# Two deformable convolution layers on one core: the order of dense tiles in the mixed stages, and the waits at the entry of the second convolution

## The reference

```python
def _deform_sample(x, offset):          # per image, tap k of 9, pixel (y, x)
    py = y + ky + off_y; px = x + kx + off_x
    # bilinear: four corners of (py, px), weights (1-|py-iy|)*(1-|px-ix|), 0 outside

# layer 0
offset = conv3x3(xn, w_off) + b_off                 # 18 channels
z = einsum('bckhw,ock->bohw', _deform_sample(xn, offset), w_dcn) + b_dcn
x = x + relu(batchnorm(z))

# layer 1, identity = xn = _gn(x)
out = gelu(batchnorm(modulated_deform_conv(xn, offset1, mask1, w_dcn1)))
out = batchnorm(modulated_deform_conv(out, offset2, mask2, w_dcn2))
x = x + gelu(out + identity)
```

## Time and profile before

| | us |
|---|---|
| three timed runs | 6902.07, 6914.19, 6914.28 |
| their median | 6914.19 |
| the profiled execution | 6903.11 |
| its span, first to last instruction | 6901.3 |
| mean granted TensorE clock in it | 0.910 of full speed |
| TensorE busy | 6028.7 |
| VectorE busy | 4828.0 |
| GpSimd busy | 4612.9 |
| ScalarE busy | 2206.3 |

### The profile page before, as it was taken

One profiled execution on the slowest core, in us unless ns is written; L12 is line 12 of the kernel. 1 busy time (PEld: TensorE's weight loads), 2 busy tenths in 40 slices (PEclk: granted clock), 3 DMA queues, 4 the chain that ended last, 5 costly groups with the idle time before them and its releaser, 6 DMA issues. The chain is left out here.

```text
span 6901.3 us, 125469 instructions
## 1 busy us (share of the span) xinstructions
PE 6028.7 (87%) x47333; PEld 4764.8 (69%) x47333; DVE 4828.0 (70%) x11440; ACT 2206.3 (32%) x3376; POOL 4612.9 (67%) x4765
## 2 busy tenths in 40 slices
PE   6987888987888887888977988789999999998996
PEld 6886677766677766676765655567777777776775
DVE  7886787866777866777864555466767776676765
ACT  1222222221222222222222222234444444443442
POOL 0006776656777757777657777767777777777776
PEclk9997998987999988999987888889999999998998
DMA  4323333334333323333322222233334333333333
GB/s 149 99 94 105 99 108 104 109 87 128 95 107 98 116 81 99 95 109 102 110 78 76 76 74 69 82 80 93 88 81 105 91 85 95 96 87 78 97 83 76
DMA packets 364107, 653.44 MB, mean 95 GB/s; under 512 B 112008, under 2 KB 270744, under 8 KB 355608
## 3 DMA queue, kind: packets, MB, share of 16 engines
q0 software_dynamic: 152064, 311.73, 18.3%
q1 hardware_dynamic: 211480, 333.92, 15.8%
HBM read 599.16 MB, written 46.15 MB: 94 GB/s over the span
## 5 line engine op out<-in xcount | busy, mean ns | idle before, releaser
L882 POOL DMA_INDIRECT G<-table,IDX x4752 | 4598.8, 968 | 2243.1 <-issue 1932.7
L2248 DVE TENSOR_TENSOR ARENA<-ARENA,OUT 128x288 f32<-128x288 f32 x2808 | 1055.5, 447 | 76.2 <-PE RED L1107 46.1
L1107 PE MATMUL RED<-IDENT,ARENA 128*96 128x128 f32 x7344 | 899.2, 283 | 88.0 <-DVE ARENA L2248 87.6
L1499 ACT ACTIVATE SAMP<-RED 96x384 f32<-96x384 f32 x688 | 334.5, 486 | 1917.1 <-PE RED L1317 812.9
L2063 DVE TENSOR_TENSOR G<-G,WPS 128x1152 f32<-128x1152 f32 x528 | 711.5, 1348 | 319.1 <-DMA G<-table,IDX 317.7
L1107 PEld LDWEIGHTS RED<-IDENT,ARENA 128*96 128x96 f32 x7344 | 831.8, 131 | 139.9 <-issue 129.2
L1298 PE MATMUL BTP<-PAD,ARENA 80*128 x2304 | 750.4, 449 | 58.2 <-issue 26.9
L1176 PE MATMUL BTP<-X 80*128 80x480 f32 x1248 | 660.2, 648 | 144.0 <-ACT X L1443 77.3
L1059 PE MATMUL OFF<-PAD,ARENA 128*54 128x128 f32 (+1 forms) x10944 | 754.2, 297 | 27.2 <-ACT PAD L1399 15.4
L1059 PEld LDWEIGHTS OFF<-PAD,ARENA 128*54 128x54 f32 (+1 forms) x10944 | 672.3, 135 | 131.3 <-issue 108.4
L1494 ACT ACTIVATE SAMP<-RED 96x384 f32<-96x384 f32 x528 | 256.9, 486 | 1559.0 <-PE RED L1195 695.0
(11 more groups left out here) (213 smaller groups left out, 7681.4 us busy)
## 6 DMA issues: line engine op xcount, KB each, us to landing
ARENA<-wtab SPq DMA_DIRECT2D x208, 800.0 KB
G<-table,IDX POOLq DMA_INDIRECT x4752
ARENA<-xo SPq DMA_DIRECT2D x96, 720.0 KB
X<-xo SPq DMA_DIRECT2D x80, 360.0 KB, 3.7
table<-TB SPq DMA_DIRECT2D x64, 384.0 KB, 2.6
X<-x SPq DMA_DIRECT2D x3, 3200.0 KB, 19.9
out<-X SPq DMA_DIRECT2D x20, 320.0 KB
wtab<-TB SPq DMA_DIRECT2D x16, 384.0 KB, 2.7
```

The source lines that it names most:

```text
L882: pool.indirect_dma_start(G[:, b, k, :], None, tables[seg.table], bass.IndirectOffsetOnAxis(ap=IDX[:, q, b * TAPS + k:b * TAPS + k + 1], a ...
L1107: last = nc.tensor.matmul(RED[b % 2][0:TPG * C, gr * 128:(gr + 1) * 128], PROD[gr][:, sft, :], IDENT[:, :], start=(sft == 0), stop=(sft == ...
L1499: nc.scalar.activation(SAMP[:, x], RED[x][0:TPG * C, 0:GROUPS * 128].rearrange("p (g n) -> p g n", g=GROUPS), ACT.Copy).then_inc(z.samp_re ...
L2248: last = nc.vector.tensor_tensor(out=PROD[gr][:, :, j * C:(j + 1) * C].rearrange("p (dy dx) c -> p dy dx c", dy=3), in0=win[:, gr:gr + 3, ...
```

## The change

MIXED_C is the pair of step lists of a mixed stage. One dense step is taken from the end of the second list and put between "x" and "f" in the first group of the first list; the number of dense tiles by which the second list starts goes from 16 to 17 accordingly. Before, the lists are xdxfd xdxfd xdxfd xdxfd and xdxdfd xdxdfd; after it, xdxdfd xdxfd xdxfd xdxfd and xdxdfd xdxdf. So the step before the norm is an "f" instead of a "d".

At the entry of C2 TensorE's wait for `base_ready` and its nine register loads go from the end of `calibrate` (before the first strip's offset convolution) to `first_strip` (behind the column transposes). The waits of ScalarE and VectorE on `x_back` go from `unlend` to `first_strip`, on ScalarE behind the first tents. SyncE's load itself stays.

```diff
-MIXED_C = "xdxfd" * 4, "xdxdfd" * 2
+MIXED_C = "xdxdfd" + "xdxfd" * 3, "xdxdfd" + "xdxdf"
...
-                    mix(on, c, MIXED_C[1], g, 12, DSEG[p + 1], 16, s, 4, "f")
+                    mix(on, c, MIXED_C[1], g, 12, DSEG[p + 1], 17, s, 4, "f")
...
                                      start=True, stop=True).then_inc(strip_turned, 1)
-                    pe.wait_ge(base_ready, 1)
-                    bases.extend(pe.value_load(BROW[0:1, 2 * k:2 * k + 1], min_val=0, max_val=(HIGHEST - LOWEST) * C) for k in range(TAPS))
                     pe.wait_ge(strip_setup, 18)
...
                 def first_strip():
-                    pass
+                    pe.wait_ge(base_ready, 1)
+                    bases.extend(pe.value_load(BROW[0:1, 2 * k:2 * k + 1], min_val=0, max_val=(HIGHEST - LOWEST) * C) for k in range(TAPS))
...
                 def unlend(halves):
-                    act.wait_ge(x_back, 16)
+                    pass
...
                 def first_strip():
                     on.tents(0, 0)
+                    act.wait_ge(x_back, 16)
...
                 def unlend(halves):
                     dve.wait_ge(weighted1, 18 * halves)
                     on.keep_range(LENT[1], 2 + halves, 2)
-                    dve.wait_ge(x_back, 16)
...
                 def first_strip():
-                    pass
+                    dve.wait_ge(x_back, 16)
```

## The result

Four runs of the changed kernel took 6857.4 to 6866.9 us, median 6861.08; four of the kernel before on the same chip had a median of 6914.23. The ratio is 0.9926, interval 0.9908 to 0.9943: the change is worth 53 us by the medians. A second measurement, further down, gave 0.9942 (0.9925 to 0.9959), 39.5 us.

What follows compares the result with a forecast made beforehand. TensorE was busiest (87% of the span), with serial chains at norm and entry. Stages -25.1 and entry -15.8 make -40.9 us: 6862.2 from the profiled run, 6873.3 from the median; 6868 was written between them, range 6848 to 6893.

Steps and rivals of the forecast that it cites:

- The tile leaves the stage ends: Ends of the three mixed stages: the norm's bn_stats starts 20.0, 19.9 and 19.0 us earlier, 58.9 us gained in all.
- one tile further on: Mixed stages: the other dense tiles each shift by one tile and no buffer changes; no cost was counted.
- The tile enters the first groups: First group of each stage, between x and f: the dense tile costs 10.9, 10.3 and 12.6 us, 33.8 in all.
- an x straight before an f leaves holes: Between x and f: TensorE idles 9.33 us without the dense tile, 7.93 with it; its clock rises from 0.88 to 0.96.
- The entry: Entry to the second convolution: the first tap comes 15.8 us earlier, with bounds 11.6 to 17.7.
- The waits: Entry, ScalarE's and VectorE's waits for X: moved behind the first strip's preparation, they let calibration start 11.6 us earlier.
- the loads: Entry, TensorE's nine register loads: the convolution starts 6.1 us earlier, but 1.9 us stay on the path before the first tap.
- Cover: Behind the norm: GpSimd's gathers for the next tile stay hidden, by 2 us for the last of four units.
- That the inserted tile costs what the removed one did: Rival, mixed stages: they give nothing and the entry's 15.8 us remain, 6898 or 6887 us; chance 0.14.
- That the entry gives nothing: Rival, entry: the first tap waits for something else, the stages' 25.1 us remain, 6878 to 6889 us; chance 0.07.
- The clock behind the longer pause: Rival, behind the norm: TensorE's clock stays at 0.50 for 50 us more per stage, 6948 us; chance 0.04.

Runs made afterwards that it cites:

- the three halves: Against the kernel before: only the new step lists, 6866.33 us; only the whole entry change, 6875.98; only the two moved waits on X, 6888.89.
- after: The first profile of the changed kernel, with lists and entry both changed against the kernel before; the profiled execution took 6857.4 us.

## Why the prediction came out right

It was right in the time (6868 forecast, 6861 measured, in the range 6848 to 6893) and in its main steps. The sum for the profiled run, -40.9 against -45.8, was 5 short, and that it came so near is in part luck: the stages gave 12.5 us more than the 25.1 forecast (by the means of three profiles 6.8 more), and the rest of C2, in which nothing was forecast, took 8.6 back.

*The tile leaves the stage ends.* The start of the norm was put at 4.6 us behind the last projection; it is 4.0 to 4.3. The sum was 58.9 us. Group 6 gives 66.2 by the means of three profiles each; 4 to 5 of the 7 us between are the shorter x in stage 2. This is the term that was off most: the other dense tiles were counted as "one tile further on" at no cost, and one of the two that prepare no offsets went from a d into an x by that. The two forms of x weren't in the rows that I read.

*The tile enters the first groups.* 33.8 us forecast; 32.7 by the stretches of the two profiles, 30.9 by group 1 in the means. All three x, d, f lie in the 82 to 87 us that were named. The price came from the same three steps elsewhere in the trace, and their neighbours are the same.

*Why it is so cheap* was told as "an x straight before an f leaves holes", with the clock rising from 0.88 to 0.96. The holes have been found: the tents that TensorE waits for, and the slow clock behind that wait. The inserted tile removes that hole from the first group, and behind the f, where the hole stays, it is 13.9 us dearer over the three stages: for the kernel as it is, the hole is the reason that the runs show. That is 4.6 us a stage, less than the 8.1 that a hole cost elsewhere; what made up the difference wasn't looked for. As a general reason the hole fell: with the holes gone the tile costs nearly the same in its group (10.2 us in stage 0), now beside a wait for gathers, and most of it is given back by the groups behind.

*The entry.* 15.8 us forecast, 16.2 measured. The waits gave 11.2 of the 11.6; the loads 5.1, where 6.1 - 1.9 = 4.2 was forecast: they begin 1 us before the end of the transposes, so TensorE's pause before the tap is 1.2 us longer than before (5.44 against 4.26) instead of 1.9. The moved waits cost nothing, and GpSimd's next tile has 12.7 of its 29.31 us left, where "some 13" was forecast.

*Cover.* The gathers behind the norm were through in time, as forecast, but more closely. The 2 us were the time from GpSimd's last gather to TensorE's first matmul of that f; by this measure 0.2 was left in stage 0 (1477.67 to 1477.83), 0.1 in stage 1 and 2.6 in stage 2. The prediction took GpSimd's end over from the trace of before, 16.9 us behind the last projection (1473.8 - 1456.85); now it is 18.2 (1477.67 - 1459.45). In stage 0 VectorE took the first unit another 2.7 us later, and it waited for no gather in any of the three.

*The rivals.* That the inserted tile costs what the removed one did: the tiles alone gave 31.5 us (by the medians), so no. That the entry gives nothing: alone it gave 21.8 by the medians, 16.2 by the timeline. The clock behind the longer pause: in stage 0 9.40 us at 0.50 and then 0.99, as before; in stages 1 and 2 the same lengths have 0.50 and 0.52, then 0.99 and 1.00.

*What stays open.* The rest of C2, with the same code behind the first tap, took 2381.6 us in the profile before, 2378.9, 2381.2 and 2387.1 in the three halves, 2390.2 in after, 2383.6 in its second profile. After lost 8.6 us there in its one profile, to a lower clock in the last 550 us whose cause isn't known. This, and the 10 us by which the stages differ with the old lists, are as large as the difference between the 39.5 and 53 us that were measured for the same change; that they are its cause wasn't tested.

## What to carry to other kernels

Price a moved step by the same step between the same neighbours, at both of its places, and list what differs in the steps that shift along with it. A hole in front of the busiest engine may hide a second lateness: when it is taken away, look at who waits next. Here an inserted step then cost no more than it did with the hole. What a step can fill is the wait of the engine that would do it, to be read from the consumer; that the producer is never idle says little.

## What the runs showed of the hardware

A wait of 4.31 us of TensorE, in the second group of stage 0, cost 8.5: the granted clock over the two steps at that place was lower (0.91 against 0.98), and the six matmuls straight behind the wait took 5.14 us instead of 3.00. That the clock would take as much again as the wait was not expected.

Nine register loads of TensorE took some 6 us at both places: 301 ns for the load itself and 0.68 us from one to the next ((4464.2 - 4458.8) / 8). The Trainium skill (DMA: Bandwidth & Descriptors, "Latency and other measured facts") gives some 600 ns as the least time of such a load. The trace doesn't show that: the load itself is shorter, and the 0.68 us hold more than the load, since the kernel's `value_load` also checks each value against its bounds (`min_val`, `max_val`); each load is followed by a register operation of 146 ns and the check.
